# Attention inside an audio tower: value products regrouped around four units, one copy placed behind an exponential, minima by reductions

## The reference, cut to what matters

```python
qkv = (x @ w_qkv.T).reshape(B, N, 3, H, hd).transpose(2, 0, 3, 1, 4)
q, k, v = qkv
q3, q4, q5 = (q[..., :g], q[..., g:2 * g], q[..., 2 * g:])      # k3..k5, v3..v5 alike
x3 = merge(_attn(q4, cat([k3, k4]), cat([v3, v4]), scale))      # _attn: softmax(q k^T scale) v
x4 = merge(_attn(q5, cat([k3, k5]), cat([v3, v5]), scale))
x5 = merge(_attn(q5, cat([k4, k5]), cat([v4, v5]), scale))
out = concatenate([x3, x4, x5], axis=2) @ w_proj.T + b_proj
h = h + out
```

## Time and profile before

| | |
|---|---|
| time, median of 3 runs | 1832.63 us (1830.71 to 1834.19) |
| profiled execution: time, span | 1832.84 us, 1831.1 us |
| PE busy in the span | 1736.6 us (95%) |
| DVE busy | 1497.6 us (82%) |
| ACT busy | 1438.5 us (79%) |
| POOL busy | 1253.9 us (68%) |

### The profile page before, as it was taken

The page is one execution under the profiler, slowest core; times in us unless marked ns, Lnnn a source line. Parts: engine busy times, 40 slices in busy tenths (PEclk is TensorE's granted clock), DMA queues, the critical chain, the costliest instruction groups (busy, mean ns, idle before and its releaser), DMA issues. The chain is left out here.

```text
span 1831.1 us, 56113 instructions
## 1 busy us (share of the span) xinstructions
PE 1736.6 (95%) x19008; PEld 1020.6 (56%) x19008; DVE 1497.6 (82%) x3546; ACT 1438.5 (79%) x2983; POOL 1253.9 (68%) x2306
## 2 busy tenths in 40 slices
PE   5999999599999999999999999999984999999999
PEld 3677777244444444444444444444443777777776
DVE  6877777689999999999999999999965555565554
ACT  4667676289999999999999999999974777777775
POOL 5677776467777777777777777777734656565651
PEclk9999999699999999999999999999997999999999
DMA  7344442144444444444444444444431333333232
GB/s 196 93 114 115 115 115 69 28 83 93 92 92 94 93 91 95 92 93 92 92 94 93 90 95 92 93 92 91 94 56 34 73 69 70 70 68 71 65 74 52
DMA packets 503935, 159.49 MB, mean 87 GB/s; under 512 B 452176, under 2 KB 503120, under 8 KB 503888
## 3 DMA queue, kind: packets, MB, share of 16 engines
q1 hardware_dynamic: 503888, 158.90, 41.0%
HBM read 37.26 MB, written 12.48 MB: 27 GB/s over the span
## 5 line engine op out<-in xcount | busy, mean ns | idle before, releaser
L753 DVE TENSOR_REDUCE tops<-p_maxa 128x6 f32<-128x762 f32 x512 | 483.6, 945 | 23.2 <-PE p_maxa L583 22.4
L660 PE MATMUL p_o<-probs,vn 127*32 127x256 f32 x6144 | 411.0, 385 | 0.4 <-DVE att L780 0.4
L703 ACT ACTIVATE probs<-p_s 128x512 f32<-128x512 f32 x512 | 305.3, 596 | 86.1 <-PE p_s L579 85.7
L757 DVE TENSOR_REDUCE tops<-p_maxb 128x4 f32<-128x508 f32 x512 | 346.3, 676 | 0.0
L579 PE MATMUL p_s<-qm,kt 32*128 32x256 f16 x3072 | 341.0, 273 | 3.0 <-DMA qm<-qk 0.7
L710 ACT ACTIVATE probs<-p_s 128x512 f32<-128x512 f32 x512 | 310.7, 607 | 2.3 <-PE p_s L579 2.2
L707 ACT ACTIVATE probs<-p_s 128x512 f32<-128x512 f32 x512 | 304.7, 595 | 0.0
L1062 DVE TENSOR_TENSOR gel_lo<-gel,gel_hi 128x512 f16<-128x512 f32 x192 | 151.7, 790 | 168.6 <-ACT gel_hi L1034 168.5
L579 PEld LDWEIGHTS p_s<-qm,kt 32*128 32x128 f16 x3072 | 135.8, 92 | 223.7 <-issue 127.0
L660 PEld LDWEIGHTS p_o<-probs,vn 127*32 127x32 f32 x6144 | 160.7, 109 | 141.0 <-issue 74.7
L808 POOL TENSOR_TENSOR qk<-raw,one 128x384 f16<-128x384 f32 x128 | 105.9, 827 | 185.4 <-ACT raw L728 185.4
(11 more groups left out here) (212 smaller groups left out, 4529.0 us busy)
## 6 DMA issues: line engine op xcount, KB each, us to landing
xt_a<-in_xt SPq DMA_DIRECT2D x32, 512.0 KB, 4.4
xt_b<-in_xt SPq DMA_DIRECT2D x64, 256.0 KB, 5.2
out<-out_sb SPq DMA_DIRECT2D x32, 336.0 KB, 2.6
xt<-hx SPq DMA_TRANSPOSE x128, 2.4
kt<-qk SPq DMA_TRANSPOSE x128, 2.8
qt<-qk SPq DMA_TRANSPOSE x128, 2.4
qm<-qk SPq DMA_TRANSPOSE x128, 2.7
yt<-ay SPq DMA_TRANSPOSE x128, 2.3
```

The source lines that it names most:

```text
L660: last = nc.tensor.matmul(p_o[32 * j:32 * j + 32, blocks, :], vn[0:NP, r, src:src + 32], probs[0:NP, r % 2, QUAD * g + j, kind * 256:(kind ...
L703: nc.scalar.activation(probs[:, r % 2, h + 1, 0:512], p_s[1][:, :, :].rearrange("p x n -> p (x n)"), ACT.Exp, scale=SCALE).then_inc(act_e1 ...
L753: nc.vector.tensor_reduce(top[:, q, 6 * pair:6 * pair + 6].rearrange("p (e k) -> p e k", e=2), p_ma[:, :, :].rearrange("p (e k) n -> p e k ...
L757: nc.vector.tensor_reduce(top[:, q, 24 + 4 * fourth:28 + 4 * fourth], p_mb[:, :, 0:NP], AX.X, ALU.max, negate=True)\
```

## The change

Three edits, all in `attend`.

First, TensorE's `outputs` calls. Before, two calls stand behind each of units 0, 1 and 3. Now there are two behind unit 0, three behind unit 1 and one behind unit 3.

Second, ScalarE's copy of `p_o` to `ot` stood in front of the three exponentials of unit 2. Now it stands behind the first of them (`exponentials` is cut into `odd` and `rest` for that, and the copy has become the function `transposed`).

Third, the minima. Two operations with two tensor operands each (L770, L771) become three reductions with one tensor operand each, over pairs that lie side by side. For that the three groups of keys are laid out in the order 3, 5, 4 (`wqkv` on the host, and the indices K3, K5, K4 in the score products).

```diff
                 products(i, r, 0)
+                outputs(i - 1, before, 0, 1)
                 outputs(i - 1, before, 0, 2)
+
+                products(i, r, 1)
                 outputs(i - 1, before, 1, 0)
-
-                products(i, r, 1)
                 outputs(i - 1, before, 1, 1)
                 outputs(i - 1, before, 1, 2)
 ...
                 outputs(i, r, 0, 0)
-                outputs(i, r, 0, 1)
 ...
-                exponentials(i, r, 0)
-
-                exponentials(i, r, 1)
-                if within(i - 1, NB):
-                    act.wait_ge(pe_pv, seen(i))
-                    nc.scalar.activation(ot[:, :, :], p_o[:, 0:3, :], ACT.Copy).then_inc(act_ot, 1)
-
-                exponentials(i, r, 2)
+                for u in range(2):
+                    odd(i, r, u)
+                    rest(i, r, u)
+
+                odd(i, r, 2)
+                transposed(i)
+                rest(i, r, 2)
 ...
-                    nc.vector.tensor_tensor(low[:, 0].rearrange("p (g j) -> p g j", g=2), of4[:, 0], of4[:, 1], ALU.min)
-                    nc.vector.tensor_tensor(low[:, 1:3], of5[:, 0:2], of5[:, 2:3].broadcast_to([128, 2, HEADS]), ALU.min).then_inc(dve_min, 1)
+                    nc.vector.tensor_reduce(low[:, 0].rearrange("p (g j) -> p g j", g=2),
+                                            got[:, 24:40].rearrange("p (j g k) -> p g j k", g=2, k=2), AX.X, ALU.min)
+                    of5 = got[:, 0:24].rearrange("p (h k) -> p h k", k=3)
+                    for pair in range(2):
+                        last = nc.vector.tensor_reduce(low[:, 1 + pair], of5[:, :, pair:pair + 2], AX.X, ALU.min)
+                    last.then_inc(dve_min, 1)
 ...
-                    maximum(p_mb[:, 0:2, :], fourth, 0, slice(0, 2), 0)
-                    maximum(p_mb[:, 2:4, :], fourth, 0, slice(0, 2), 1).then_inc(pe_mb[u], 1)
+                    maximum(p_mb[:, 0:2, :], fourth, 0, slice(K3, K4 + 1, 2), 0)
+                    maximum(p_mb[:, 2:4, :], fourth, 0, slice(K3, K4 + 1, 2), 1).then_inc(pe_mb[u], 1)
 ...
-    arr["wqkv"] = np.concatenate([w[:, C // 3:2 * C], v], axis=1)
+    k3, k4, k5 = (w[:, C + x * C // 3:C + (x + 1) * C // 3] for x in range(3))
+    arr["wqkv"] = np.concatenate([w[:, C // 3:C], k3, k5, k4, v], axis=1)
```

More of the change, by code:

```diff
@@ L459, in attend @@
         K0 = NQ * 32
+        K3, K5, K4 = range(3)
         scaled, moved = sb("scaled", [128, C]), sb("moved", [128, 1])
@@ L598, in odd @@
                     if do:
-                        score(p_s[1][:, 2:4, :], b, 1, slice(0, 3, 2)).then_inc(pe_s1[u], 1)
+                        score(p_s[1][:, 2:4, :], b, K4, slice(0, 3, 2)).then_inc(pe_s1[u], 1)
                         pe.wait_ge(act_e5[u - 1] if u else act_e5[3], seen(i + 1 if u else i))
-                        score(p_s5[:, 0:2, :], fifth, 2, slice(1, 3), 0)
-                        score(p_s5[:, 2:4, :], fifth, 2, slice(1, 3), 1).then_inc(pe_half[u], 1)
+                        score(p_s5[:, 0:2, :], fifth, K5, slice(1, 3), 0)
+                        score(p_s5[:, 2:4, :], fifth, K5, slice(1, 3), 1).then_inc(pe_half[u], 1)
                 if has_s:
@@ L607, in products @@
                     pe.wait_ge(act_e1[u - 1] if u else act_e1[3], seen(i + 1 if u else i))
-                    score(p_s[1][:, 0:2, :], b, 0, slice(0, 2))
+                    score(p_s[1][:, 0:2, :], b, K3, slice(0, 2))
                 if u == 2:
@@ L616, in products @@
                     pe.wait_ge(act_e0[u - 1] if u else act_e0[3], seen(i + 1 if u else i))
-                    score(p_s[0][:, 0:2, :], a, 0, slice(0, 2))
-                    score(p_s[0][:, 2:4, :], a, 1, slice(0, 3, 2)).then_inc(pe_s0[u], 1)
+                    score(p_s[0][:, 0:2, :], a, K3, slice(0, 2))
+                    score(p_s[0][:, 2:4, :], a, K4, slice(0, 3, 2)).then_inc(pe_s0[u], 1)
                 if has_m:
                     pe.wait_ge(dve_mb[u - 1], seen(i + 2 if u < 3 else i + 3))
-                    maximum(p_mb[:, 0:2, :], fourth, 0, slice(0, 2), 0)
-                    maximum(p_mb[:, 2:4, :], fourth, 0, slice(0, 2), 1).then_inc(pe_mb[u], 1)
+                    maximum(p_mb[:, 0:2, :], fourth, 0, slice(K3, K4 + 1, 2), 0)
+                    maximum(p_mb[:, 2:4, :], fourth, 0, slice(K3, K4 + 1, 2), 1).then_inc(pe_mb[u], 1)
             def rows(o, x, name, bias=None):
@@ L698, in _, with transposed, odd @@
         def _(act):
-            def exponentials(i, r, u):
+            def transposed(i):
+                if within(i - 1, NB):
+                    act.wait_ge(pe_pv, seen(i))
+                    nc.scalar.activation(ot[:, :, :], p_o[:, 0:3, :], ACT.Copy).then_inc(act_ot, 1)
+            def odd(i, r, u):
                 if within(i, NB):
@@ L704, in exponentials, with rest @@
                                          scale=SCALE).then_inc(act_e1[u], 1)
+            def rest(i, r, u):
+                if within(i, NB):
+                    h = 2 * u
                     act.wait_ge(pe_half[u], seen(i + 1))
@@ L730, in body @@
                                          p_z[:, 320:512].rearrange("p (s d) -> p s d", d=G8), ACT.Copy).then_inc(act_v, 1)
-                exponentials(i, r, 3)
+                odd(i, r, 3)
+                rest(i, r, 3)
             loop(act, body)
@@ L766, in body @@
                     got = top[:, (r + 1) % 2]
-                    of5 = got[:, 0:24].rearrange("p (h k) -> p k h", k=3)
-                    of4 = got[:, 24:40].rearrange("p (j g k) -> p k g j", g=2, k=2)
                     low = slots((r + 1) % 2, 0, NQ)[:, :, 24].rearrange("p (x h) -> p x h", x=3)
-                    nc.vector.tensor_tensor(low[:, 0].rearrange("p (g j) -> p g j", g=2), of4[:, 0], of4[:, 1], ALU.min)
-                    nc.vector.tensor_tensor(low[:, 1:3], of5[:, 0:2], of5[:, 2:3].broadcast_to([128, 2, HEADS]), ALU.min).then_inc(dve_min, 1)
+                    nc.vector.tensor_reduce(low[:, 0].rearrange("p (g j) -> p g j", g=2),
[4 more added lines that the diff above has]
+                    last.then_inc(dve_min, 1)
                 maxima(i, r, 2)
```

## The result

The changed kernel takes 1876.65 us (median of 4 runs, 1876.17 to 1878.34), the kernel before 1831.97 in the same comparison (4 runs, 1830.71 to 1834.19): a ratio of 1.024, with an interval of 1.0224 to 1.0255. It is slower by 44.7 us. The forecast was 1884. The profiled run took 1876.74 us, span 1875.0.

A forecast was written before the change was run, and what follows sets the result against it. It took a closed loop of waits through TensorE and VectorE (7.77 us), with another close behind, as the bound. Value products add 0.43 us over 118 rounds, 51 us on 1832.8: 1884 us, range 1862 to 1892.

The forecast's parts named there:

- The ring through VectorE: Closed wait loop through TensorE's unit 2, VectorE's reciprocal to unit 0's maxima, unit 1's end: 7.77 us, becoming 8.20 us.
- 0.43 us a round: Price of one value-product group added on TensorE between units 1 and 2, claimed to lengthen every round in full.
- TensorE goes through the unit, `qkv` and the three transposes without a stop: Reading of TensorE from unit 2's start at 902.82 to the transposes' end at 905.05: no waits inside.
- The sentence that priced the DMAs of query and key rows at nothing: GpSimd and these DMAs start 0.31 us later in a round 0.43 longer, claimed to cost nothing.
- The count of 118: Of 128 rounds, 118 counted at full price, since the first and last fill and drain the pipeline.
- The copy: ScalarE's copy to `ot` behind unit 2's first exponential: projection starts 3.10 us behind unit 2 instead of 2.79.
- the second ring: Wait loop through value products, copy, unit 2's exponentials, projection and unit 0's exponentials: 8.08 us after the change.
- The minima: VectorE's three reductions cost 0.27 to 0.88 us, hidden in the wait for unit 2's maxima: no time saved.
- TensorE's busy time of some 93 of 100: Sign expected in the attention: TensorE's busy time falls to this from 98.6 without being faster.
- VectorE as the bound with minima that pay: Rival, chance 0.06: VectorE sets the pace, reductions give 0.25 us a round back, 30 us in all: 1803 us.
- a TensorE that is simply full: Rival, chance 0.05: TensorE at 98.6% has the same work in another order, so time stays 1833 us.
- the second ring alone: Rival, chance 0.15: VectorE's loop is shorter than read, round 8.08 us, 0.29 longer, 34 us in all: 1867 us.

The follow-up runs named there:

- e7: e1 with VectorE's batch statistics moved from between unit 3's and unit 0's maxima to behind the minima; 1843.31 us, ratio 1.0055.
- e1: Kernel before with only the value products in their new places, copy and minima as before; 1867.36 us, ratio 1.0176.
- e2: Kernel before with only the copy to `ot` moved behind unit 2's first exponential; 1867.6 us, ratio 1.0178.
- e9: Changed kernel with VectorE's batch statistics moved to behind the minima; 1867.59 us, ratio 1.0188.
- e3: Kernel before with only the minima as three reductions and the key group order they need; 1831.76 us, ratio 0.9993.
- e10: Changed kernel with the two old minima operations and old key group order, so value products and copy moved alone; 1875.26 us, ratio 1.0239.
- e6: Changed kernel with one more group of value products moved: two behind unit 0, four behind unit 1, none behind unit 3; 1921.72 us, ratio 1.0485.

## Why the prediction was right, and where it was off

**The ring through VectorE: right.** Its signs are in the rows above: the block of 24, the 1.43 to unit 2, the last maxima 0.06 behind the end of unit 0's reductions, and that over all rounds of the stretch. The round is 8.14 instead of 8.20. e7 shows that shortening the ring by a VectorE instruction shortens the round. In the kernel before, this ring set only some of the rounds (44 of 103) and the second one the others; the prediction, which read one round, had the two a few hundredths apart.

**0.43 us a round: too large; 0.35 was measured.** The block did grow by 0.43. The step that failed is "TensorE goes through the unit, `qkv` and the three transposes without a stop". In the kernel before unit 2 did stop, some 0.13 of its 0.63, for the query rows; matmuls of scores run beside that wait, so TensorE shows no idle time, and the stop is only seen in the distance from the unit to `qkv` and in the DMA's landing. The term of the sum that this makes too large is the price of the group, 0.43, taken to stay whole in the round. The sentence that priced the DMAs of query and key rows at nothing is the same mistake: 0.31 later in a round that is 0.43 longer is 0.12 earlier for unit 2. What arrives earlier shortens the unit, and a shorter unit makes the round, and with it the gain, smaller: 0.43 - x longer, 0.12 - x earlier, and x is what is given back; x = 0.06. Measured is 0.06 (0.625 - 0.564, the means of the table with one more digit). The ring is then 7.77 + 0.43 - 0.06 = 8.14. In e1, without the copy's delay, the whole 0.13 comes back, and the round is 8.07.

**The count of 118: right for this sum.** 41.2 us between first and last minima are 118 x 0.35. The forecast of 1884 is 7 us too high and not 51 - 41.2 = 10, since 43.9 - 41.2 = 2.7 us lie outside these rounds, for which the sum has no term; that they make the miss smaller is luck.

**The copy: right.** The projection starts 908.10 - 905.02 = 3.08 behind unit 2, forecast 3.10; the second ring is 8.066 in e2 and e9, forecast 8.08. It ended 0.07 under the first ring, which hides it in the changed kernel but for the later query rows: that is the 0.07 between e1's round and the changed kernel's.

**The minima: right.** 0.34 us for three (904.71 to 905.05), inside the 0.27 to 0.88, and no time from it (e3, e10).

**TensorE's busy time of some 93 of 100: wrong.** It is 97.0, since the same rows overlap less and cover more time (section on the result). ScalarE's idle ahead of unit 2's first exponential was 0.70, forecast 0.9.

**The rivals.** VectorE as the bound with minima that pay is excluded by e3; a TensorE that is simply full by e7, which has e1's program on TensorE and takes 24 us less; the second ring alone is what e2 and e9 are, not the changed kernel. Left open: the ring's terms, read to a hundredth, leave a few hundredths a round that no row places; that the two rings take turns in the kernel before is one likely part of it, which no run here separates.

## What to carry to other kernels

When three engines are nearly full, look for the ring: follow from one instruction what it waited for, through the single buffers, back to itself one round later; work moved into the ring costs its length, less what waits inside the ring give back, even if the engine's total work stays (0.43 us of 0.43 from e1 to e6, 0.29 in e1). Look for a second ring close behind, because two edits that each lengthen another ring do not add, and relieving one only uncovers the other. And compare the same stretch of an engine with its shortest form elsewhere, since a wait beside running matmuls is not shown as idle (here 0.13 us a round).

## What the runs showed of the hardware

- A VectorE operation with two tensor operands took from 194 to 557 ns (L770); in e1, where it falls beside another part of GpSimd's work, it never took over 211. The first of the reductions with one tensor operand (L778) took 190 to 197 ns in all 98 rounds, the others (L782) 175 to 183. The Trainium skill ("SBUF — State Buffer", section "SBUF: two separate sides") has it that of a GpSimd operation that reads SBUF and a VectorE one with two SBUF inputs the one that starts later is blocked for the whole of the other; these rows agree.
- A duration is not a pace: ScalarE's exponentials at 907.78, 908.26 and 908.74 last 0.66 to 0.69, others 0.60, and start 0.48 apart all the same (0.48 to 0.50 between exponentials of 0.60).
- TensorE's busy time is not its work: in the attention the rows add up to 4300 us in both kernels, and the time that they cover rose from 979 to 1004 us.
- A DMA that turns the query rows took 2.4 us from issue to landing, and the matmuls that wait for it started 0.10 us behind the landing.
